# Rank products of a feed-forward group behind the eighth instead of the seventh first-layer step of the next group

## The chip, the cores and the metric

The kernel runs on one core of a Trainium2 chip. Five engines work side by side, each with its own queue in which instructions go in order: TensorE (PE: matrix products; weight loads are shown as PEld), VectorE (DVE), ScalarE (ACT), GpSimd (POOL) and SyncE (SP), which here only issues transfers. They wait for each other by semaphores. The metric is the time of one execution on the device in microseconds (us), and the median over several executions is compared.

## What is computed

The input is a graph with 1250 nodes of 512 features and 40000 edges. Cut to what matters:

```python
xn = _layernorm(x)
x = x + gnn(xn, W1, b1, W2, b2, eps, src, dst) + mix(xn)      # graph layer and attention
x = x + ffn(_layernorm(x))                                    # 16 experts, top 2

# gnn:  rst = (1 + eps) * feat + segment_sum(feat[src], dst)
#       h = relu(rst @ W1 + b1) @ W2 + b2;  return h + feat        (512 -> 1024 -> 512)
# ffn:  logits = xt @ router_w.T + router_b;  probs = softmax(logits)
#       topk_p, topk_i = top_k(probs, 2)
#       out = sum over experts e of gate_e * (gelu(xt @ w1e.T + b1e) @ w2e.T + b2e)
```

The change lies in the two dense layers of the graph layer, called the feed-forward here, and in the routing to the experts that is done beside them.

## The kernel before

The 1250 nodes are ten tiles of 128 rows. The kernel goes through stages: layer norm and projections, attention with the graph sums, the output projection, the feed-forward of the graph layer (about 438 to 567 us of the profiled execution), the rest of the routing, a loop over the experts' tiles, and the sum at the end. Every instruction's place in its queue is written out by hand, so the order on an engine is that of the code.

The feed-forward takes the tiles in four groups, FC_TILES: tiles 0 to 2, 3 to 5, 6 and 7, 8 and 9. For each group TensorE does the first layer in eight steps m = 0 to 7 (KH = 8), one for each 128 of the 1024 hidden features. A step is twelve products at line 1456: four slices of 128 inputs, three products each, since numbers are split into a high and a low part. They have 384, 256 or 226 columns, by the size of the group. A step writes one of four PSUM banks in turn and signals hid_ps. ScalarE makes h_32 and h_hi from it (lines 758 and 759), VectorE makes h_lo (line 1094). Then mix(t) does the second layer of a tile, 24 products of 512 columns at line 1399, which takes the h_lo of each step for the group's first tile. VectorE adds the result to the row (line 1107) and normalises it (lines 1109 to 1114), TensorE turns the normalised tile (turn_x2n, line 1408) and multiplies it by the router's weights (route, line 1417).

The routing of a group f - 1 is done during the first layer of group f, in pieces between the steps:

- TensorE does the last turning and router products behind steps 1 and 3.
- VectorE does pick(f - 1) behind the h_lo of step 4: sixteen small operations in a chain (lines 1021 to 1037), each waiting for the one before it. They find the two best experts of each row and write them to mask16. Line 1040 signals mask_ready.
- ScalarE does the exponents (line 744) behind step 5.
- TensorE does ranks(f - 1) at line 1424: small products that count, for each row and expert, how many earlier rows chose that expert. The first of them waits for mask_ready, the last signals rank_ps.
- VectorE does place, tally and weigh behind the h_lo of step 7. The first operation of place, line 1050, waits for rank_ps. Place writes the slots and signals slots_ready, on which GpSimd waits with its scatters (line 628). Tally updates seen, which the next ranks read.

The routing of the last group, tiles 8 and 9, has no steps beside it. It follows the last mix, and the expert loop follows that. SyncE loads eight experts' weights in the meantime: four when hid_ps has counted all 32 steps, four when mix_ps has counted ten tiles. It reads the first rows from the slots (line 457) when the scatters have landed.

Of the kernel before, what the change touches and what calls it, by code (L numbers as in the profile page):

```python
# [37 lines left out]
KH = HID // P  # L38
# [36 lines left out]
def layer(nc, x, src, dst, wqkv, wo, bo, gw1, gb1, gw2, gb2, geps, rw, rb, ew, eb1, eb2, out):  # L75
# [10 lines left out]
    with ExitStack() as ctx:  # L86
# [389 lines left out]
        def _(pool):  # L476
# [134 lines left out]
            for _, what, i in sorted([(start(max(w - 4, 0)), "cols", w) for w in range(NW)]  # L611
                                     + [(min(6 * (p + 1), RAW) + 0.5, "split", p) for p in range(2)]
                                     + [(summed[w // WPG], "spare", w) for w in range(0, NW, 2)]):
                {"cols": window_columns, "spare": spare_chunks, "split": split_pair}[what](i)
# [588 lines left out]
        def _(pe):  # L1203
# [91 lines left out]
            for g, (which, p, b) in enumerate(projections):  # L1295
                o, n = BLOCKS[b]
# [91 lines left out]
            def mix(t, first, hidden):  # L1388


                r = rows(t)
                c = (t - first) * P
                if t >= 2:
                    pe.wait_ge(x2_ready, t - 1)
                for m in range(KH):
                    if t == first:
                        pe.wait_ge(hid_lo, hidden + m + 1)
                    for i, (h, w) in enumerate(((h_hi, w2_hi[:, m, :]), (h_lo, w2_hi[:, m, :]), (h_hi, w2_lo[:, m, :]))):
                        ins = pe.matmul(bank[4 + t % 2][0:r, :], h[:, m, c:c + r], w,  # L1399
                                        start=(m == 0 and i == 0), stop=(m == KH - 1 and i == 2))  # L1400
                ins.then_inc(mix_ps, 1)

            def turn_x2n(t):
                pe.wait_ge(x2n_ready, t + 1)
                if t:
                    pe.wait_ge(x2nt_saved, t)
                for k in range(KD):
                    ins = pe.transpose(bank[6][:, k * P:(k + 1) * P], x2n[:, t, k * P:(k + 1) * P], ident[:, :])
                ins.then_inc(x2nt_ps, 1)

            def route(t):
                pe.wait_ge(x2nt_saved, t + 1)
                f = sum(1 for tiles in FC_TILES if tiles[-1] < t)
                if f and t == FC_TILES[f][0]:
                    pe.wait_ge(slots_ready, f)
                for k in range(KD):
                    ins = pe.matmul(bank[7][:, t * EXP:(t + 1) * EXP], x2n_t[:, t % 2, k, :], rw_sb[:, k, :],
                                    start=(k == 0), stop=(k == KD - 1))
                ins.then_inc(logit_ps, 1)

            def ranks(f):

                def ahead(to, of, mask, start, stop):
                    return pe.matmul(bank[7][:, to * EXP:(to + 1) * EXP], of[:, :], mask, start=start, stop=stop,
                                     skip_group_check=True)

                tiles = FC_TILES[f]
                masks = [mask16[:, t * EXP:(t + 1) * EXP] for t in tiles]
                pe.wait_ge(mask_ready, f + 1)
                for i, t in enumerate(tiles):  # L1430
                    ahead(NT + t, ones, seen[:, :], True, False)
                    for mask in masks[:i]:
                        ahead(NT + t, ones, mask, False, False)
                    ins = ahead(NT + t, tri, masks[i], False, True)
                if tiles[-1] == NT - 1:
                    ahead(2 * NT, ones, seen[:, :], True, False)
                    for mask in masks:
                        ins = ahead(2 * NT, ones, mask, False, mask is masks[-1])
                ins.then_inc(rank_ps, 1)
# [4 lines left out]
            for f, tiles in enumerate(FC_TILES):  # L1444
                o = tiles[0] * P
                n = min(N, tiles[-1] * P + P) - o
                for m in range(KH):
                    if g < 4:
                        pe.wait_ge(out_added, 4 + g)
                    else:  # L1450
                        pe.wait_ge(hid_hi, g - 3)
                    if g == 0 or g == KH // 2:
                        pe.wait_ge(w1_lo_ready, KD if g == 0 else 2 * KD)
                    for k in range(KD):
                        for i, (w, r) in enumerate(((w1_hi, rst_hi), (w1_hi, rst_lo), (w1_lo, rst_hi))):
                            ins = pe.matmul(bank[g % 4][:, 0:n], w[k][:, m * P:(m + 1) * P], r[k][:, o:o + n],  # L1456
                                            start=(k == 0 and i == 0), stop=(k == KD - 1 and i == 2))
                    ins.then_inc(hid_ps, 1)
                    g += 1

                    if o and m == 1:
                        turn_x2n(tiles[0] - 1)
                        route(tiles[0] - 2)
                    if o and m == 3:
                        route(tiles[0] - 1)
                    if o and m == 6:
                        ranks(f - 1)
                pe.wait_ge(w2_lo_ready, KH)
                pe.wait_ge(out_added, NT)
                for t in tiles:  # L1470
                    mix(t, tiles[0], g - KH)
                    if t - 1 in tiles:
                        turn_x2n(t - 1)
                    if t - 2 in tiles:
                        route(t - 2)
# [106 lines left out]
```

## Time and profile before

| | |
|---|---|
| Median of 3 runs | 740.73 us |
| Lowest and highest | 739.47 and 741.41 us |
| Profiled execution: time | 739.14 us |
| Profiled execution: span of the instructions | 737.4 us |
| Busy share of the span: TensorE, VectorE, ScalarE, GpSimd | 93%, 64%, 32%, 21% |
| Mean granted clock of TensorE | 0.972 of full |

The profile is of one execution. Its times are microseconds from the start of the span, so two places are compared by subtracting their starts. The time of an execution is its span plus 1.7 us around it. A busy share is an average over stages that are bound by different things, and what a stall costs is read at its own place: what the engine waits for, and what had stood ready to run. In the timeline a bracket behind a row gives the engine's idle time ahead of it and what ended it.

### The profile page before, as it was taken

To read this page: it belongs to the slowest core of one execution; us is meant where nothing else is said; L and a number is where in the kernel's file an instruction comes from. 1 tells how busy PE (TensorE), PEld (TensorE's weight loads), DVE (VectorE), ACT (ScalarE), POOL (GpSimd) and SP (SyncE) were. 2 spreads that over 40 slices of the span, in tenths; PEclk is the share of its full clock that TensorE was granted. 3 is DMA by queue.
4 is the path that set the end of the run, shared out by engine and by line. 5 is a ranking of instruction groups with operands and counts; after the bars stand their busy time and mean duration, and the time that the engine had idled before them with its cause. 6 is when DMAs were issued, how large, how long until landed. Compare 5 with 4: busy or idle time off the path is not lost.

```text
span 737.4 us, 12476 instructions
## 1 busy us (share of the span) xinstructions
PE 683.9 (93%) x3860; PEld 453.2 (61%) x3861; DVE 474.6 (64%) x1065; ACT 233.5 (32%) x472; POOL 155.9 (21%) x262
## 2 busy tenths in 40 slices
PE   4889999999999999999999999999898299999997
PEld 2545545455655565555555789898886176777742
DVE  5629752389888898887964997344445634445536
ACT  2222311223233232332333435160542243354320
POOL 6045210103133331312300700003112212232210
PEclk9999999999999999999999999999999589999978
DMA  9700000072543717090735920002018668844458
GB/s 292 212 0 0 1 3 1 0 288 102 204 171 133 258 46 286 22 342 30 276 137 184 382 112 1 1 1 87 17 70 315 263 205 300 307 142 127 130 201 301
DMA packets 48198, 109.70 MB, mean 149 GB/s; under 512 B 6694, under 2 KB 6710, under 8 KB 45680
## 3 DMA queue, kind: packets, MB, share of 16 engines
q1 hardware_dynamic: 38480, 85.41, 32.4%
q0 software_dynamic: 4256, 13.41, 4.9%
q10 hardware_dynamic: 5376, 9.93, 4.4%
q8 instruction: 31, 0.51, 0.3%
q14 instruction: 55, 0.45, 0.2%
HBM read 47.39 MB, written 61.35 MB: 147 GB/s over the span
## 4 chain that ended last, share of the span: by engine, by line
PE 80%; DVE 9%; DMA 3%; issue 3%; ACT 1%; POOL 1%; SPq 1%; DVEq 0%; ACTq 0%; POOLq 0%
PE bank L1361 12%; PE bank L1344 10%; PE bank L1312 8%; PE bank L1399 8%; PE bank L1278 7%; PE bank L1456 6%; PE bank L1522 6%; PE bank L1508 6%; PE bank L1323 5%; PE bank L1242 4%; PE bank L1384 4%; DMA arena<-in_x 2%; DVE arena L918 2%; PE bank L1532 2%; PE bank L1483 1%
## 5 line engine op out<-in xcount | busy, mean ns | idle before, releaser
L918 DVE TENSOR_TENSOR arena<-iota,arena 125x384 f16<-125x384 f16 (+2 forms) x318 | 172.6, 605 | 23.3 <-PE bank L1242 14.0
L718 ACT ACTIVATE arena<-bank 128x416 f32<-128x416 f32 (+1 forms) x120 | 62.2, 518 | 147.0 <-PE bank L1344 144.0
L1361 PE MATMUL bank<-arena 128*64 128x416 f32 (+1 forms) x480 | 97.2, 524 | 3.3 <-DVE arena L971 2.8
L971 DVE TENSOR_SCALAR arena<-bank 128x416 f32<-128x416 f32 (+1 forms) x120 | 67.5, 589 | 42.8 <-PE bank L1344 42.7
L554 POOL COPY arena<-arena 125x12 f32 (+1 forms) x80 | 35.2, 440 | 229.1 <-DVE arena L918 122.7
L1312 PE MATMUL bank<-arena 128*128 128x416 f32 (+1 forms) x192 | 75.8, 544 | 2.6 <-ACT arena L656 1.4
L1242 PE MATMUL bank<-arena 125*128 125x160 f16 x471 | 51.5, 234 | 5.7 <-DVE arena L918 5.2
L1508 PEld LDWEIGHTS bank<-arena 128*128 128x128 f32 x448 | 52.8, 194 | 6.2 <-issue 6.2
L1312 PEld LDWEIGHTS bank<-arena 128*128 128x128 f32 x192 | 36.7, 200 | 30.1 <-issue 26.7
L1242 PEld LDWEIGHTS bank<-arena 125*128 125x128 f16 x471 | 32.5, 98 | 36.8 <-issue 27.1
L1361 PEld LDWEIGHTS bank<-arena 128*64 128x64 f32 x480 | 30.6, 135 | 36.5 <-issue 26.7
L1508 PE MATMUL bank<-arena 128*128 128x128 f32 x448 | 52.9, 277 | 0.0
L1522 PE MATMUL bank<-arena 128*128 x112 | 50.4, 593 | 0.0
L628 POOL DMA_INDIRECT slots<-arena,slot x20 | 19.9, 996 | 140.1 <-DVEq L1057 135.2
L1153 DVE COPY arena<-arena 128x1024 f32 x30 | 20.9, 696 | 44.4 <-issue 40.2
L1344 PE MATMUL bank<-q_hi,k_hi 64*128 64x416 f32 (+1 forms) x240 | 48.7, 402 | 0.4 <-ACT arena L700 0.4
L638 POOL DMA_INDIRECT expert_rows<-arena x28 | 27.5, 980 | 97.6 <-DVE arena L1187 93.3
L1344 PEld LDWEIGHTS bank<-q_hi,k_hi 64*128 64x128 f32 x240 | 22.2, 181 | 39.3 <-issue 38.5
L1278 PE MATMUL bank<-xn_hi,a_t 128*128 128x512 f32 x100 | 45.5, 455 | 0.0
L1344 PE MATMUL bank<-q_lo,k_hi 64*128 64x416 f32 (+1 forms) x240 | 42.5, 350 | 0.0
L1344 PE MATMUL bank<-q_hi,k_lo 64*128 64x416 f32 (+1 forms) x240 | 42.4, 348 | 0.0
L1456 PE MATMUL bank<-rst_hi,w_hi 128*128 128x384 f32 (+2 forms) x128 | 40.3, 315 | 0.0
(247 smaller groups left out, 1183.6 us busy)
## 6 DMA issues: line engine op xcount, KB each, us to landing
slots<-arena SPq DMA_DIRECT2D x6, 5397.0 KB, 17.8
arena<-in_ew SPq DMA_DIRECT2D x16, 1024.0 KB, 6.0
slots<-arena SPq DMA_DIRECT2D x2, 5140.0 KB, 17.0
arena<-slots ACTq DMA_DIRECT2D x28, 257.0 KB, 3.0
arena<-in_x SPq DMA_DIRECT2D x8, 512.0 KB, 7.2
arena<-in_gw SPq DMA_DIRECT2D x2, 2048.0 KB, 17.0
arena<-in_wqkv SPq DMA_DIRECT2D x3, 1024.0 KB, 15.3
xn_rows<-arena SPq DMA_DIRECT2D x1, 2560.0 KB, 8.4
```

What stands on the lines that cost most here:

```text
L718: act.activation(probs[0:kt, s % NPB, 0, 0:n], bank[2 * (s % 2)][0:kt, 0:n], ACT.Relu).then_inc(p0_ready, 1)
L918: ins = dve.tensor_tensor(hot[:, :, c], iota16[0:CE, 0:width].unsqueeze(1).to_broadcast([CE, n, width]), window_cols[:, i % WBUF, of, k0:k ...
L971: dve.tensor_single_scalar(probs[0:kt, s % NPB, 1, 0:n], bank[2 * (s % 2) + 1][0:kt, 0:n], 0.0, op=ALU.max).then_inc(p1_ready, 1)
L1242: return pe.matmul(window_at(w), of[:, at_slot:at_slot + P], of[:, at_slot + P:at_slot + OHW], start=start, stop=stop, skip_group_check=True)
L1278: ins = pe.matmul(bank[NB][:, :], a_t[:, g % 2, t, :], x[t][:, :], start=(t == 0 and x is xn_hi), stop=(t == NT - 1 and x is xn_lo), skip_ ...
L1312: ins = pe.matmul(bank[g % 5][:, 0:n], w_qkv[:, part, k, c:c + P], xn_t[:, k, o:o + n], start=(k == 0), stop=(k == KD - 1))
L1344: ins = pe.matmul(bank[2 * (s % 2) + a][0:kt, 0:n], k[p][half, t * P:t * P + kt], q[p][half, o:o + n], start=(i == 0), stop=(i == len(term ...
L1361: ins = pe.matmul(bank[AV][DH * a:DH * a + DH, 0:n], v_sb[0:kt, t, h * DH:h * DH + DH], probs[0:kt, s % NPB, a, 0:n], start=(t == 0), stop ...
L1399: ins = pe.matmul(bank[4 + t % 2][0:r, :], h[:, m, c:c + r], w, start=(m == 0 and i == 0), stop=(m == KH - 1 and i == 2))
L1456: ins = pe.matmul(bank[g % 4][:, 0:n], w[k][:, m * P:(m + 1) * P], r[k][:, o:o + n], start=(k == 0 and i == 0), stop=(k == KD - 1 and i == 2))
L1508: ins = pe.matmul(bank[a][:, m * P:(m + 1) * P], w1_now[:, a, k * DFF + m * P:k * DFF + m * P + P], xg_t[:, a, k, :], start=(k == 0), stop ...
L1522: ins = pe.matmul(bank[6 + a][:, :], hg_t[:, a, k, :], arena[:, bass.ds(lies[a] + KD * DFF + k * D, D)], start=(k == 0), stop=(k == KF - 1))
```

## The change

```diff
@@ -1463,7 +1463,7 @@
                         route(tiles[0] - 2)
                     if o and m == 3:
                         route(tiles[0] - 1)
-                    if o and m == 6:
+                    if o and m == KH - 1:
                         ranks(f - 1)
                 pe.wait_ge(w2_lo_ready, KH)
                 pe.wait_ge(out_added, NT)
```

The call of ranks(f - 1) goes from behind the seventh step (m = 6) to behind the eighth (m = 7). That happens at three places, in the first layers of the groups of tiles 3 to 5, 6 and 7, and 8 and 9 (o is zero in the first group, which has no ranks to do). The orders of VectorE, ScalarE, GpSimd and SyncE stay word for word the same.

TensorE at the first place, tiles 3 to 5. The names rst_hi, rst_lo, w_hi and w_lo are the parts of the inputs and of the first layer's weights; a bracket names the semaphores that a row waits for. Rows with a minus stand there in the kernel before.

```order
 L1456 MATMUL bank<-rst_lo_109,w_hi_97 128x384
 L1456 MATMUL bank<-rst_hi_105,w_lo_101 128x384
-L1424 MATMUL bank<-seen,ones 128x16 [waits mask_ready]
-L1424 MATMUL bank<-mask,tri 128x16
-L1424 MATMUL bank<-seen,ones 128x16
-L1424 MATMUL bank<-mask,ones 128x16
-L1424 MATMUL bank<-mask,tri 128x16
-L1424 MATMUL bank<-seen,ones 128x16
-L1424 MATMUL bank<-mask,ones 128x16 x2
-L1424 MATMUL bank<-mask,tri 128x16
 L1456 MATMUL bank<-rst_hi_102,w_hi_94 128x384 [waits hid_hi]
 L1456 MATMUL bank<-rst_lo_106,w_hi_94 128x384
```

The ranks stood between the last product of the seventh step and the first of the eighth, which itself waits only for hid_hi.

TensorE at the third place, tiles 8 and 9, now, behind the twelve products of the eighth step. Rows with a plus are new there; w_hi and h_hi of line 1399 are the second layer.

```order
 L1456 MATMUL bank<-rst_lo_109,w_hi_97 128x226
 L1456 MATMUL bank<-rst_hi_105,w_lo_101 128x226
+L1424 MATMUL bank<-seen,ones 128x16 [waits mask_ready]
+L1424 MATMUL bank<-mask,tri 128x16
+L1424 MATMUL bank<-seen,ones 128x16
+L1424 MATMUL bank<-mask,ones 128x16
+L1424 MATMUL bank<-mask,tri 128x16
 L1399 MATMUL bank<-w_hi,h_hi 128x512 [waits x2_ready,hid_lo,out_added,w2_lo_ready]
 L1399 MATMUL bank<-w_hi,h_lo 128x512
```

The ranks and their wait now stand ahead of the second layer. The second place is moved in the same way.

VectorE at the first place, the same in both kernels: the end of pick, the h_lo of steps 5, 6 and 7, and the start of place.

```order
L1037 TENSOR_TENSOR mask<-arena 128x48 [waits dve_chain]
L1094 TENSOR_TENSOR h_lo<-arena,h_hi 128x384 [waits dve_chain,hid_hi]
L1094 TENSOR_TENSOR h_lo<-arena,h_hi 128x384 [waits hid_hi] x2
L1050 TENSOR_TENSOR arena<-bank,ebase 128x48 [waits rank_ps]
L1051 TENSOR_TENSOR arena<-arena 128x48 [waits dve_chain]
```

Place stands behind the h_lo of the eighth step, so it waits for that step as well as for the ranks.

## Rows read from the trace of the kernel before

**Rows 1.** The page: its first line, and the shares of the chain of waits.
```profile
span 737.4 us, 12476 instructions
...
PE 80%; DVE 9%; DMA 3%; issue 3%; ACT 1%; POOL 1%; SPq 1%; DVEq 0%; ACTq 0%; POOLq 0%
```

**Rows 2.** Who waited for whom, TensorE, 485 to 590 us (total, times, longest).
```profile
PE bank L1424 <- DVEq L1040: 8.2, 4, 3.7
```

**Rows 3.** Timeline, TensorE, first place (start, us, engine, line, operation, [idle before <-releaser]).
```profile
490.84 0.34 PE L1456 MATMUL bank<-rst_hi,w_lo 128*128 128x384 f32 x1
492.04 0.18 PE L1424 MATMUL bank<-seen,ones 128*128 128x16 bf16 x1 [0.86 <-DVEq L1040]
...
492.27 0.42 PE L1456 MATMUL bank<-rst_hi,w_hi 128*128 128x384 f32 x1
...
494.46 0.40 PE L1399 MATMUL bank<-w_hi,h_hi 128*128 128x512 f32 x1
```

**Rows 4.** Timeline, VectorE, first place.
```profile
491.71 0.21 DVE L1037 TENSOR_TENSOR mask<-arena 128x48 bf16<-128x48 f32 x1
...
495.75 0.56 DVE L1094 TENSOR_TENSOR h_lo<-arena,h_hi 128x384 fp32r<-128x384 f32 x1 [2.49 <-ACT h_hi L759]
496.22 0.20 DVE L1050 TENSOR_TENSOR arena<-bank,ebase 128x48 f32<-128x48 f32 x1
```

**Rows 5.** Timeline, TensorE, second place.
```profile
524.90 0.28 PE L1456 MATMUL bank<-rst_hi,w_lo 128*128 128x256 f32 x1
527.07 0.18 PE L1424 MATMUL bank<-seen,ones 128*128 128x16 bf16 x1 [1.89 <-DVEq L1040]
...
527.32 0.36 PE L1456 MATMUL bank<-rst_hi,w_hi 128*128 128x256 f32 x1
...
528.82 0.40 PE L1399 MATMUL bank<-w_hi,h_hi 128*128 128x512 f32 x1
```

**Rows 6.** Timeline, TensorE, third place.
```profile
551.98 0.28 PE L1456 MATMUL bank<-rst_hi,w_lo 128*128 128x226 f32 x1
553.99 0.18 PE L1424 MATMUL bank<-seen,ones 128*128 128x16 bf16 x1 [1.73 <-DVEq L1040]
...
554.13 0.35 PE L1456 MATMUL bank<-rst_hi,w_hi 128*128 128x226 f32 x1
...
555.55 0.41 PE L1399 MATMUL bank<-w_hi,h_hi 128*128 128x512 f32 x1
```

**Rows 7.** Timeline behind the last second-layer product, all engines.
```profile
566.91 0.69 DVE L1107 TENSOR_TENSOR arena<-arena,bank 98x512 f32<-98x512 f32 x1 [2.65 <-PE bank L1399]
...
587.58 1.48 SPq L457 DMA_DIRECT2D arena<-slots  x2
...
590.32 1.08 PE L1483 MATMUL bank<-ident,arena 128*128 128x128 f32 x4 [9.89 <-DMA arena<-slots]
```

**Rows 8.** Busy time of each engine in 1 us windows; PEclk is the granted clock.
```profile
569.00:570.00 1.00, 0.15 (x2) 0.09 (x2) 0.71 (x2) 0.07 (x1) 0.00 (x0) 0.93 0.94 390
...
593.00:594.00 1.00, 1.00 (x7) 1.00 (x7) 0.06 (x1) 0.40 (x1) 0.00 (x0) 0.62 0.08 16
```

**Rows 9.** Timeline, TensorE, around the two changes of the clock.
```profile
567.99 1.06 PE L1417 MATMUL bank<-rw_sb,arena 128*128 128x16 f32 x8 [0.69 <-ACT arena L770]
...
571.71 1.89 PE L1417 MATMUL bank<-rw_sb,arena 128*128 128x16 f32 x8 [0.69 <-ACT arena L770]
...
592.56 4.31 PE L1508 MATMUL bank<-arena 128*128 128x128 f32 x32
```

**Rows 10.** Chain of waits (start, us, what): second layer, expert loop, end.
```profile
494.62 11.10 PE bank L1399 x48
...
619.88 3.57 PE bank L1508 x32
...
719.11 3.73 PE bank L1546 x4
...
724.31 0.69 DVE arena L1199
```

## The prediction

> **What bounds the kernel now.** I read the page first. The chain of waits, followed back from the last instruction, lies 80% on TensorE and only 9% on VectorE [rows 1]. So TensorE is what a change has to make shorter, and what matters is where TensorE stands still. The next view is therefore the list of who waited for whom, for TensorE alone, from 485 us, in the first layer of tiles 3 to 5, to the expert loop. Its largest entry is line 1424, the rank products, which waited four times, 8.2 us in all, and the longest wait was 3.7 us [rows 2]. What released them was VectorE's queue at line 1040, the signal at the end of pick. The longest of the four is that of the last ranks, those of tiles 8 and 9, which have no step behind them and are not touched by the change. That leaves about 4.5 us for three waits, and the timelines show them: 0.86, 1.89 and 1.73 us of idle time ahead of the first rank product [rows 3, 5, 6].
>
> These three stalls are a real loss and not slack that something else covers. Between the waits TensorE runs without a gap: the last product of the seventh step starts at 490.84, then nothing starts until 492.04, although the eighth step (line 1456) needs nothing from pick. It stands behind the rank products only because the queue is in order. Behind it the second layer (line 1399) starts at 494.46 and keeps the array busy for 11.10 us, 48 products without a gap [rows 10].
>
> **The change part by part.** Nothing is added or removed. At three places, in the first layer of tiles 3 to 5, of tiles 6 and 7 and of tiles 8 and 9, the rank products (eight, eight and five rows of the order) move from ahead of the eighth first-layer step to behind it. The wait on mask_ready moves with them. On VectorE, ScalarE, GpSimd and SyncE the order stays. So each place is a matter of three times: when the seventh step ends, when the mask is there, and how long the eighth step takes.
>
> First place, tiles 3 to 5. The last product of the seventh step starts at 490.84 and its successors follow each other about 0.175 us apart: from 492.27 to 494.46 are twelve products, of which the first has some 0.1 us more. So TensorE could have gone on at 491.02. It went on at 492.04 [rows 3], a stall of 1.02 us. With the change the eighth step starts at 491.02 and needs 2.09 us, to 493.11. The last operation of pick runs from 491.71 to 491.92 [rows 4], so the mask is there 1.1 us before the rank products come up, and they wait for nothing. The gain is the whole stall: **1.02 us**.
>
> Second place, tiles 6 and 7. The seventh step's last product starts at 524.90, and TensorE is free at 525.02. The ranks started at 527.07, 2.05 us later. The eighth step lasts 1.50 us from 527.32 to 528.82 [rows 5], of which 0.08 is the slower start after a pause. It now ends at 526.44, and the mask comes at the same time as before, since what pick waits for (line 1094 of the fifth step and the router products ahead of it) isn't moved. So 0.63 us of waiting are left. The ranks then run from 527.07 and take 0.25 us, and the second layer starts at 527.32 to 527.40 where it was 528.82. The gain is not the stall but the length of the step put into it: **1.42 us**.
>
> Third place, tiles 8 and 9. TensorE is free at 552.09, the ranks start at 553.99, and the step goes from 554.13 to 555.55 [rows 6]. The step has 1.34 us without its slow start. It ends at 553.43, 0.56 us of waiting are left, and the second layer starts at 554.13 to 554.21. Gain: **1.34 us**.
>
> The sum is 1.02 + 1.42 + 1.34 = 3.78 us. If the slow start of 0.08 us isn't paid by the second layer, it is 3.94, so I take **3.8 us**.
>
> **What could become late instead.** Four things hang on the moved products or on the step.
> Place (line 1050) waits for the ranks. At the first place these end 1.1 us later than before, at about 493.4 us. But VectorE did not come to line 1050 before 496.22, since the h_lo of the eighth step stands ahead of it and was made at 495.75 [rows 4]. That h_lo now comes 1.3 us earlier, because the step no longer stands behind stall and ranks: still about 1.4 us behind the ranks. The cover holds. At the other two places the ranks start when they did, so nothing is later.
> The second layer's first tile takes h_lo step by step. It takes the eighth h_lo seven steps behind its start, and a step has three products of 11.10 / 48 = 0.23 us [rows 10], so 4.8 us behind it, by my reckoning at 498.1 at the first place. The h_lo is there at about 495.0. Were this cover gone, every microsecond would be paid by TensorE.
> The eighth step uses the bank that the fourth step's ScalarE reads have left long before.
> The slots come from place, and with it the scatters of GpSimd. Both get earlier.
>
> Downstream, the gain has to come through to the end. Behind the last second-layer product the chain goes over VectorE (line 1107 had stood idle for 2.65 us waiting for TensorE, at 566.91), the routing of the last tiles, the scatters, and then SyncE's read of the slots at 587.58, for which TensorE stood idle 9.89 us until 590.32 [rows 7]. All these wait for products that now end 3.8 us earlier. So do the first eight loads of expert weights: SyncE issues them at the last hid_ps and the last mix_ps. I find no transfer that starts by another event than these and ends in this stretch, so the whole tail should slide. Nothing new is hidden or uncovered by it.
>
> **The clock.** The granted clock is 2.4 GHz at the three places and falls to 1.2 GHz during the window from 569 to 570 us (mean 0.93 there), after pauses of TensorE in the routing of the last tiles. It rises again in the window from 593 to 594 (mean 0.62) [rows 8]. The eight router products took 1.06 us ahead of the fall and 1.89 behind it [rows 9]. The stalls that the change removes were at full clock and cost no clock, so none is won back there.
> The Trainium skill (TensorE: Matmul & The Clock Gate, Part 1: The HAM clock gate) says that the gate looks at activity in windows that run freely, not in step with the kernel. By that rule the slide of the work against the windows may let the fall and the rise meet other products. The trace neither confirms nor denies it, as it shows one execution.
>
> **The rivals.**
> *Full gain* (the forecast): 3.8 us, 740.73 - 3.8 = 736.9.
> *Absorbed gain.* The end is set somewhere behind by something that doesn't move, as a transfer of weights or rows in the tail. For it speaks that TensorE waits 9.89 us for the slots' read [rows 7] and that transfers are in the chain with 3% [rows 1]. Against it speaks that I find an event of TensorE or VectorE ahead of each of them. A partial form: only the first stall's 1.02 us or only half of the sum comes through. That gives 738.8 to 740.7.
> *Slower by the clock.* The mechanism is one: the low level holds more of the work behind 567 us than now. Its price from rows: thirty-two products of the expert loop take 3.57 us at the full clock [rows 10], 4.31 when the rise falls among them [rows 9], and would take about 7.1 entirely at the low level: 2.8 us more. An earlier fall would take the router products of the tile before it with it, 1.89 - 1.06 = 0.83 more [rows 9]. At the end two tiles of line 1546 take 3.73 us at the low level [rows 10], 1.86 each, while behind the rise the chain lies on VectorE, with two operations of about 0.69 for a tile, one of which is shown. Eight tiles kept low cost 8 x (1.86 - 1.38) = 3.8 us. All together 7.4 us, so 740.73 - 3.8 + 7.4 = 744.3. It decides for slower only from 6.0 us on, since 3.8 must be eaten first and 2.2 are 0.3%. It needs all three places at once. One alone only makes the gain smaller, and the opposite case (a late fall, 0.8 us, or an early rise, 0.7 us) makes it larger.
> *The change does nothing.* It would need that TensorE already runs the eighth step during the wait. The starts at 490.84 and 492.04 with nothing between exclude it [rows 3].
>
> **How the numbers follow.** The sum is made against the profiled execution: span 737.4, time 739.14, which gives 733.6 and 735.3. That execution lies 1.6 us under the median of the runs shown, 740.73. The runs themselves span 739.47 to 741.41, which I read as the size of what the clock and the transfers do by chance, about 1 us to each side. For the median I take 740.73 - 3.8 = 736.9. Chances: full gain, with that scatter, 0.84. Absorbed in part or whole, 0.12. Slower by the clock, 0.04. A measurement of this kernel can tell about 0.3%, 2.2 us, from no change: faster means under 738.5, slower over 742.9. From the full case a small part with an unlucky clock falls within 0.3%, and a part of the absorbed case ends under 738.5, and the two about cancel. A little of the slow case stays under 742.9 too. So faster 0.84, same 0.13, slower 0.03. The range goes from 734.9 (the sum of 3.94, with 1.9 us more from an early rise, a late fall and the scatter of the runs) to 739.2, which takes in half of the absorbed case.
>
> **What the changed kernel's profile would show.** At the first place the rank products without idle time ahead of them, behind the twelve products of the eighth step; in the second and third an idle time of about 0.6 us ahead of the ranks. The wait list of TensorE for line 1424 should fall from 8.2 us to 3.7 + 0.6 + 0.6 = 4.9. The second layers should start at 493.4, 526.3 and 551.7 us (the earlier gains taken off: 1.0 at the second, 2.4 at the third), and the last second-layer product should end at 563.1. The place of line 1050 should still be released by VectorE's own order and not by line 1424. The prediction is wrong in its core if the second layer starts as early as this and the span doesn't follow, and wrong in the sum if the mask comes later than before relative to the fifth step.

## The result

The changed kernel takes 735.29 us (median of 5 runs, 732.79 to 737.21), the kernel before 740.73 us (median of 5, 739.47 to 743.22). The ratio is 0.9917 with a 95% interval of 0.9892 to 0.9943, so the change saves 4.2 to 8.0 us, with 5.4 between the medians. The forecast was 3.8 us, with a range of 734.9 to 739.2 us. The direction was right, and the local mechanism too, but the size lies above it: 3.8 us would be a ratio of 0.9949, just outside the interval, and the ratio of 0.9917 on 740.73 us gives 734.6, just under the range, though the median itself lies in it. Medians and intervals leave out executions more than 1.5% above the fastest of their kernel, which is a single one, of 756.32 us in e2.

The page of the changed kernel, its first line and the shares of the chain of waits, beside [rows 1]:

```profile
span 735.5 us, 12476 instructions
...
PE 80%; DVE 8%; DMA 4%; issue 3%; ACT 1%; POOL 1%; ACTq 1%; SPq 0%; DVEq 0%; POOLq 0%
```

The profiled execution (737.21 us) is the longest of its five, and the profiled one of before (739.14) was the shortest seen until then. Their spans differ by 1.9 us only. Which of the two numbers, 1.9 or 5.4, the change made is what the rest is about.

TensorE's waits from 485 to 590 us, beside [rows 2]:

```profile
PE bank L1424 <- DVEq L1040: 4.6, 3, 3.7
```

8.2 us in four waits have become 4.6 in three, and the 3.7 of the last tiles are still among them. The forecast was 4.9.

The executions already differ ahead of the change. To compare, one needs a place that both share, and I take the first product of the second layer of tiles 0 to 2, which the change does not touch. In the kernel before:

```profile
455.56 0.50 PE L1399 MATMUL bank<-w_hi,h_hi 128*128 128x512 f32 x1 [0.29 <-DVE w_lo L1091]
```

TensorE in the changed kernel, the same place and then the three places of the change, beside [rows 3, 5, 6]:

```profile
456.35 0.50 PE L1399 MATMUL bank<-w_hi,h_hi 128*128 128x512 f32 x1 [0.29 <-DVE w_lo L1091]
...
493.92 0.18 PE L1424 MATMUL bank<-seen,ones 128*128 128x16 bf16 x1
...
494.16 0.48 PE L1399 MATMUL bank<-w_hi,h_hi 128*128 128x512 f32 x1
...
526.86 0.18 PE L1424 MATMUL bank<-seen,ones 128*128 128x16 bf16 x1 [0.45 <-DVEq L1040]
...
527.12 0.47 PE L1399 MATMUL bank<-w_hi,h_hi 128*128 128x512 f32 x1
...
552.36 0.18 PE L1424 MATMUL bank<-seen,ones 128*128 128x16 bf16 x1 [0.39 <-DVEq L1040]
...
552.58 0.48 PE L1399 MATMUL bank<-w_hi,h_hi 128*128 128x512 f32 x1
```

The changed execution is 456.35 - 455.56 = 0.79 us late before it comes to the change. That taken off, the second layers start at 493.37, 526.33 and 551.79, where they started at 494.46, 528.82 and 555.55: earlier by 1.09, 2.49 and 3.76 us, which is 1.09, 1.40 and 1.27 us for the three places. The forecast was 1.02, 1.42 and 1.34. At the first place the ranks no longer wait, at the other two the rest of the wait is there. The first product of the second layer now takes 0.48 or 0.47 us where it took 0.40, so this layer pays for the slower start behind the ranks.

VectorE at the first place, beside [rows 4]:

```profile
492.51 0.21 DVE L1037 TENSOR_TENSOR mask<-arena 128x48 bf16<-128x48 f32 x1
...
495.20 0.56 DVE L1094 TENSOR_TENSOR h_lo<-arena,h_hi 128x384 fp32r<-128x384 f32 x1 [1.14 <-ACT h_hi L759]
495.67 0.20 DVE L1050 TENSOR_TENSOR arena<-bank,ebase 128x48 f32<-128x48 f32 x1
```

Place still comes behind the h_lo of the eighth step, 1.4 us behind the ranks' end at about 494.2, and waits for nothing else. The cover that the prediction named holds.

Behind the second layer, all engines, beside [rows 7]:

```profile
564.01 0.69 DVE L1107 TENSOR_TENSOR arena<-arena,bank 98x512 f32<-98x512 f32 x1 [2.65 <-PE bank L1399]
...
584.68 1.48 SPq L457 DMA_DIRECT2D arena<-slots  x2
...
587.46 1.09 PE L1483 MATMUL bank<-ident,arena 128*128 128x128 f32 x4 [9.92 <-DMA arena<-slots]
```

From the common place to this addition it is 107.66 us, and was 111.35: **3.69 us** saved, the 3.76 less that slower start. From the addition to the read of the slots it is 20.67 us in both, so the stretch behind slides as a whole. The gain that can be seen in the two traces is thus 3.7 us. The rest of the way the two executions differ by things that the change does not touch: 0.79 us at the start, 0.09 less up to the expert loop, 0.68 more in the loop and 0.41 more behind it. The sum, 0.79 - 3.69 - 0.09 + 0.68 + 0.41, is the -1.9 us of the spans.

So two questions were left: where single executions get their noise of several microseconds, and why the medians say more than 3.7.

### The profile page after: what moved, and what is told of

It reads as the page before. It is cut to its first block, busy times and chain, and to the rows that moved or that the text cites. A ratio compares the mean times of both kernels' runs of the same rounds, so it can differ in the third digit from the quotient of the medians.

```text
span 735.5 us, 12476 instructions
## 1 busy us (share of the span) xinstructions
PE 685.5 (93%) x3860; PEld 453.7 (62%) x3861; DVE 473.5 (64%) x1065; ACT 233.7 (32%) x472; POOL 153.4 (21%) x262
## 4 chain that ended last, share of the span: by engine, by line
PE 80%; DVE 8%; DMA 4%; issue 3%; ACT 1%; POOL 1%; ACTq 1%; SPq 0%; DVEq 0%; POOLq 0%
PE bank L1361 12%; PE bank L1344 10%; PE bank L1312 9%; PE bank L1399 8%; PE bank L1278 7%; PE bank L1456 6%; PE bank L1522 6%; PE bank L1508 5%; PE bank L1323 5%; PE bank L1242 4%; PE bank L1384 4%; DMA arena<-slots 2%; DVE arena L918 2%; DMA arena<-in_wqkv 2%; PE bank L1532 2%
## 5 line engine op out<-in xcount | busy, mean ns | idle before, releaser
L918 DVE TENSOR_TENSOR arena<-iota,arena 125x384 f16<-125x384 f16 (+2 forms) x318 | 169.7, 593 | 23.3 <-PE bank L1242 14.0
L554 POOL COPY arena<-arena 125x12 f32 (+1 forms) x80 | 33.3, 417 | 230.8 <-DVE arena L918 136.1
L1312 PEld LDWEIGHTS bank<-arena 128*128 128x128 f32 x192 | 37.3, 203 | 31.0 <-issue 27.3
```

Source lines behind the costliest of these rows:

```text
L918: ins = dve.tensor_tensor(hot[:, :, c], iota16[0:CE, 0:width].unsqueeze(1).to_broadcast([CE, n, width]), window_cols[:, i % WBUF, of, k0:k ...
L1312: ins = pe.matmul(bank[g % 5][:, 0:n], w_qkv[:, part, k, c:c + P], xn_t[:, k, o:o + n], start=(k == 0), stop=(k == KD - 1))
```

## The experiments

Theory A says that the gain is 3.7 us and the rest chance. Theory B says that the expert loop gives a surplus. Theory C came up with the second experiment: TensorE's stalls cost clock as well as time. Each comparison is with runs of the kernel before on the same chip in the same job.

**e1, the changed kernel once more.**

> The changed kernel once more, to see how firm its gain of 5.4 us (median) is. Theory A (the gain is the 3.8 us at the three places and the rest is chance, since the first reads of rows in the expert loop land late by different amounts from execution to execution): 3 to 5 us under the kernel before, a profile whose second layers start 1.0 to 1.1, 2.4 to 2.5 and 3.7 to 3.8 us earlier relative to the first layer's start. Theory B (the change also spares about 2 us in the expert loop): again 5 to 6 us under it, with the first passes of the loop shorter in the profile than in the kernel before.

Measured: 736.73 us (8 runs, 733.82 to 740.44) against 741.17 (15 runs), ratio 0.9929 (0.9901 to 0.9957), so 4.4 us between the medians. The profile has the same local times: 107.69 us from the common place to the addition. But it is a long execution, with a span of 738.7 us, and its chain of waits shows two things. It comes to the common place 2.0 us later than that of before (457.51), and the reads of rows in the expert loop are late. The chain in the loop, start, time, what; first e1, then the first changed execution:

```profile
597.46 3.44 PE bank L1522 x8
...
607.51 8.04 DMA arena<-slots
...
616.70 4.62 PE bank L1522 x8
```

```profile
592.01 3.00 DMA arena<-slots
...
605.99 6.31 DMA arena<-slots
...
623.23 6.10 DMA arena<-slots
```

A read of rows takes 3.0 us ahead of the loop and 6.1 to 8.0 us when SyncE loads expert weights of 1 MB beside it. Then the pass waits. A pass without a wait is 7.88 us long; over the loop's thirteen intervals the excess is 2.1 us in the profile of before, 2.8 in the changed one and 4.7 in e1. That speaks against theory B, under which the changed kernel's loop would be shorter, and names one source of noise. Another is the common place itself, which comes anywhere between 454.5 and 458.3 us in the profiles.

The wait costs e1 clock as well. TensorE stood idle for 2.80 us ahead of the pass at 615.6 us, and the granted clock is low over that pass, so the eight products at 616.70 take 4.62 us instead of 3.44:

```profile
614.00:616.00 2.00, 0.41 (x2) 0.42 (x3) 0.17 (x1) 0.00 (x0) 0.00 (x0) 0.89 0.16 66
616.00:618.00 2.00, 2.00 (x6) 1.17 (x5) 0.65 (x1) 0.60 (x1) 0.00 (x0) 0.50 0.82 211
```

**e4, the changed kernel with the loads of weights spread over the passes.**

```diff
-            for e in (6, 7, 8, 11, 12, 13, 14, 15):
+            for i, e in enumerate((6, 7, 8, 11, 12, 13, 14, 15)):
+                if i:
+                    sp.wait_ge(y_ps[1], i)
                 expert(e)
```

> The changed kernel with the expert weights that are loaded during the expert loop spread over the passes: each load after the first waits for the end of one more pass's last product. The reads of rows then don't share the transfer engines with 1 MB loads. Theory A: the reads land in about 3 us instead of 6 to 7, no pass of the loop is longer than 7.9 us, 1.5 to 3 us under the changed kernel, and the runs lie within 2 us where those of the changed kernel lay within 4.4. Rival (the reads are late for another reason): passes of about 9 us remain and the time stays.

Measured: 731.96 us (5 runs, 731.55 to 733.26), ratio 0.9873 (0.9839 to 0.9906), 4.8 us under e1. All passes are 7.88 us long, and no transfer is left in the chain of the loop:

```profile
595.38 3.44 PE bank L1524 x8
598.81 3.57 PE bank L1510 x32
602.38 0.87 PE bank L1485 x8
603.26 3.44 PE bank L1524 x8
```

The gain is larger than the 1.5 to 3 us expected, and fits e1's profile with its 4.7 us of excess better than the first one with 2.8. The runs lie within 1.7 us, those of e1 within 6.6. The late reads came from the loads beside them.

**e2, the ranks one step earlier (unspread).** It is the opposite of the change: `if o and m == 5:`.

> The ranks one step earlier than in the kernel before, behind the sixth step (m = 5). Theory A: each stall grows by one step, 2.09 + 1.42 + 1.34 = 4.85 us, and all of it reaches the end: 740.7 + 4.9 = about 745.6. In the profile the idle times ahead of the ranks are about 3.0, 3.4 and 3.1 us. Rival (something behind the feed-forward takes up the slide): less than 3 us. Theory B: more than 6 us.

Measured: 748.52 us (7 runs), 7.4 over the kernel before; the ratio, 1.0087 (1.0056 to 1.0118), gives 6.4, or 4.2 to 8.7. The middle lies above theory A's 4.85 and at theory B's 6, but the interval still takes in 4.85. What decides is the profile. TensorE at the first place, and the granted clock around it (the column third from the end, 1.00 for 2.4 GHz and 0.50 for 1.2):

```profile
491.99 0.20 PE L1424 MATMUL bank<-seen,ones 128*128 128x16 bf16 x1 [2.96 <-DVEq L1040]
...
499.14 0.39 PE L1399 MATMUL bank<-w_hi,h_hi 128*128 128x512 f32 x1
```

```profile
488.00:490.00 2.00, 1.03 (x6) 0.71 (x5) 1.66 (x7) 0.95 (x3) 0.00 (x0) 1.00 0.00 0
490.00:492.00 2.00, 0.01 (x1) 0.02 (x2) 1.63 (x10) 1.65 (x3) 0.00 (x0) 0.79 0.00 0
492.00:494.00 2.00, 2.00 (x15) 2.00 (x16) 0.56 (x1) 0.00 (x0) 0.00 (x0) 0.50 0.03 8
...
498.00:500.00 2.00, 2.00 (x12) 1.88 (x11) 0.12 (x1) 0.66 (x2) 0.00 (x0) 1.00 0.00 0
```

The stall is the expected one, 2.96 us. But during it the clock goes from 2.4 to 1.2 GHz and stays there until 498 us, so the next step and most of the one behind it run at half speed. From the common place to this second layer it is 43.63 us instead of 38.90: 4.7 us for a step of 2.1. At the other two places it is 2.9 and 2.8 us for 1.4 and 1.3, with the clock low from about 532 and 563 us. Each stall of 3 us cost 1.5 to 2.6 us more than itself. That is theory C: it was not among the prediction's rivals for these places.

**e3, the ranks one step later.** They go into mix(t), behind the first three products of the group's first tile.

```diff
-                    if o and m == KH - 1:
-                        ranks(f - 1)
@@ in mix(t, first, hidden, f)
+                    if t == first and first and m == 0:
+                        ranks(f - 1)
```

> The ranks one step later than in the changed kernel, behind the first three products of the second layer's first tile, at the same three places. Theory A: the idle times of 0.45 and 0.39 us that the changed kernel's profile shows ahead of the ranks at the second and third place are covered by these products (0.69 us), so 0.8 us under the changed kernel. Rival (place on VectorE now waits for the ranks): idle time ahead of line 1050's operation with the ranks as its releaser, and no gain or a loss.

Measured: 735.15 us (6 runs), ratio 0.9916 (0.9883 to 0.9949), 1.6 under e1, which the intervals don't separate. In the profile the waits are gone at all three places. The second one, TensorE:

```profile
525.58 0.40 PE L1399 MATMUL bank<-w_hi,h_hi 128*128 128x512 f32 x1
...
526.29 0.18 PE L1426 MATMUL bank<-seen,ones 128*128 128x16 bf16 x1
```

From the common place to the addition it is 106.44 us, 1.2 less than in the changed kernel. 0.84 of them are the two waits.

**e5 and e6, the kernel before and the changed one, both with spread weights.** The loop's noise is taken out of the comparison.

> The kernel before with the same spread of the expert weights as in e4. The passes of the expert loop are then equal in both kernels, and the difference to e6 is that of the moved ranks alone. Theory A (only the stalls count): 3.7 us over e6, as the profiles say. Theory C (a stall of 2 us of TensorE lets its clock fall in some executions, as one of 3 us did in e2): 4 to 6 us over e6, and among the runs some with a mean clock lower by 0.002 to 0.004 that are longer by 1 to 3 us. Rival B (the loop gave the surplus): the difference is 3.7 and the runs lie close together.

> The kernel of e4 once more, on the chip of e5. All theories: 731.5 to 732.5 us on this scale, with all passes of the loop 7.88 us long and runs within 2 us.

Measured: 737.60 us (9 runs, 736.22 to 739.09) and 733.04 (6 runs, 729.87 to 734.93); ratios to the kernel before 0.9918 (0.9889 to 0.9946) and 0.9853 (0.9813 to 0.9893). The change is worth 4.6 us between the medians and 4.8 between the means, and by the scatter of the two sets of runs the latter is 3.2 to 6.4. So 3.7 is not excluded by this pair. The loop cannot give a surplus here, as all its passes are 7.88 us long in both profiles, so rival B is out. The mean clock of the runs is 0.9704 in e5 and 0.9720 in e6, a difference within their scatter. And e5's profile shows the full clock at all three places, so theory C was not shown yet. The runs of e6 spread over 5 us, more than the 2 expected, and their median is 0.5 us over the expected 731.5 to 732.5.

**e7 and e8, spread weights with the ranks later, and earlier.**

> Ranks behind the first three products of the second layer (as e3) and spread weights (as e4). The local gain of e3's profile over the changed kernel's, 1.2 us between the first second layer and the last add, should now be visible in the time: 1.2 us under e6 (0.8 from the idle times, the rest from fewer slow starts). If the median is within 0.4 us of e6, the local gain doesn't come through.

> Ranks behind the sixth step (as e2) and spread weights (as e4). Theory A alone: 4.85 us over e5. Theory C: e2's profile lost 2.6, 1.5 and 1.5 us more at the three places, since the clock fell behind each stall of 3 us, so 9 to 10.5 us over e5, and a mean clock lower by 0.006 to 0.01.

Measured: e7 730.96 us (6 runs, 729.32 to 735.25), ratio 0.9839 (0.9797 to 0.9881). It is 2.1 us under e6 by the medians and 1.2 by the means, and 1.35 by the traces (106.44 against 107.79 us from the common place to the addition). The interval does not exclude that it is no better than e6. e8 747.67 us (12 runs), 10.1 over e5, where the local stalls alone would be 4.85; its mean clock is 0.962. Its profile has a low clock behind each of the three stalls of 2.96, 3.31 and 3.07 us. Theory C holds for stalls of 3 us, in six of six cases with e2.

**e9 to e12, between the two, and place by place.** e9 has the ranks in the middle of the seventh step, e10 is e5 again, e11 keeps only the first place's stall, e12 only the other two.

```diff
@@ e9: in the loop over k of line 1456's products, behind them
+                        if o and m == 6 and k == 1:
+                            ranks(f - 1)
@@ e11
-                    if o and m == 6:
+                    if o and m == (6 if f == 1 else 7):
@@ e12
-                    if o and m == 6:
+                    if o and m == (7 if f == 1 else 6):
```

> Spread weights, and the ranks in the middle of the seventh step (behind its second slice of inputs). Each stall is half a step longer than in e5: about 2.1, 2.8 and 2.6 us. The local sum without any fall of the clock is 1.05 + 0.71 + 0.67 = 2.4 us over e5. Theory A: that. Theory C (stalls of 2 to 3 us let the clock fall in a part of the executions): 4 to 6 us over e5, a mean clock between those of e5 and e8, and a profile in which one or two of the three stalls are followed by a stretch at the low clock.

> The kernel of e5 once more on this chip, as the ground for e9, e11 and e12. 737 to 738.5 us. Theory C: with stalls of 1.0, 2.1 and 1.9 us a fall behind one of the last two stands in some profiles; the chance that this one shows it is about a third to a half.

> Spread weights, and the ranks moved at the second and third place only, so that the first place keeps its stall of 1.0 us. Locally 2.6 us under e10 (1.40 + 1.27). Theory A: 2.6 under it. Theory C: the surplus hangs on the two stalls of 2 us, so 3.5 to 4.5 under e10 and a mean clock as of e6 (0.972).

> Spread weights, and the ranks moved at the first place only, so that the second and third keep their stalls of 2.1 and 1.9 us. Both theories: 1.1 us under e10, since the stall of 1.0 us costs only itself. Under theory C the mean clock stays that of e5 and e10 (0.970). A gain of 2 us or more here would say that the surplus sits at the first place.

| | median us (runs) | ratio to before | mean clock | common place to addition |
|---|---|---|---|---|
| e10 | 739.01 (12) | 0.9957 (0.9922 to 0.9991) | 0.968 | 111.47 |
| e9 | 740.22 (12) | 0.9972 (0.9937 to 1.0007) | 0.970 | 115.32 |
| e11 | 731.76 (6) | 0.9850 (0.9805 to 0.9894) | 0.976 | 108.69 |
| e12 | 735.89 (8) | 0.9916 (0.9877 to 0.9956) | 0.972 | 110.51 |

The traces give what was expected of the places: e12 saves 0.96 us, e11 saves 2.78. The times say more, 3.1 and 7.3 us, which neither theory expected. The expectation of e12 had named a sign for a gain of 2 us or more: that the surplus sits at the first place, with its stall of 1.0 us. The 3.1 us are such a gain, but with this scatter they are 1.0 to 5.1, and no profile shows a fall behind that stall. e10 itself came out 1.4 us over e5, the same kernel, and its twelve runs reach from 736.2 to 745.7 us, so part of these two differences may be e10's.

e11 and e12 can be compared without e10. They differ in which stalls they keep, e11 the first and e12 the other two, and e12 takes 4.1 us more by the medians and 4.3 by the means (2.7 to 5.9), where the traces give 110.51 - 108.69 = 1.8. Its mean clock is 0.972 against 0.976. So the executions with the two stalls of 2 us lose more than the stalls, and show a lower clock, although the one profile of e12 has no fall at either place. How much of the clock's difference lies at these places is not shown: in the two profiles the low stretch behind the routing of the last tiles also differs, 23.9 us in e12 and 20.5 in e11.

In e9 the 3.85 us of the trace are 2.4 of longer stalls and one fall of the clock, behind the stall of 2.60 us at the second place; behind those of 1.91 and 2.41 us there is none. By the medians e9 is only 1.2 us over e10, less than either theory said. The runs of e9 fall apart in two: seven with a mean clock of 0.972 to 0.975 take 738.1 to 740.5 us, five with 0.963 to 0.967 take 741.8 to 745.4.

e9, the granted clock behind the stall of 2.60 us:

```profile
526.00:528.00 2.00, 0.00 (x0) 0.00 (x0) 1.72 (x11) 1.59 (x3) 0.00 (x0) 1.00 0.00 0
528.00:530.00 2.00, 1.50 (x18) 1.50 (x19) 0.77 (x3) 0.20 (x1) 0.00 (x0) 0.87 0.00 0
530.00:532.00 2.00, 2.00 (x11) 2.00 (x11) 0.43 (x1) 0.64 (x2) 0.00 (x0) 0.50 0.00 0
```

**e13 to e16, four further profiles of e5's kernel.** What was left was whether the stalls of 2 us, those that the kernel before has, do it too.

> A profile of the kernel of e5. Theory C: in about a third of such profiles the granted clock is low for some microseconds right behind the ranks of the second or third place, the second layer behind it starts 1 to 2 us later, and the time is over 739 us. Rival (chance elsewhere): full clock there in every profile; long executions are long at the start, in the routing of the last tiles or at the end.

> As e13, a further profile: theory C a fall behind a stall of 2 us in one of three, the rival none.

> As e13, a further profile: theory C a fall behind a stall of 2 us in one of three, the rival none.

> As e13, a further profile: theory C a fall behind a stall of 2 us in one of three, the rival none.

They do in all four profiles, where theory C expected one in about three. TensorE and the granted clock in e13, at the second place:

```profile
526.54 0.18 PE L1426 MATMUL bank<-seen,ones 128*128 128x16 bf16 x1 [1.90 <-DVEq L1042]
...
528.53 0.63 PE L1401 MATMUL bank<-w_hi,h_hi 128*128 128x512 f32 x1
```

```profile
524.00:526.00 2.00, 0.64 (x6) 0.44 (x4) 1.72 (x11) 1.97 (x5) 0.00 (x0) 1.00 0.00 0
526.00:528.00 2.00, 1.46 (x19) 1.47 (x20) 1.15 (x4) 0.39 (x2) 0.00 (x0) 0.99 0.00 0
528.00:530.00 2.00, 2.00 (x8) 1.71 (x7) 0.36 (x2) 1.22 (x3) 0.00 (x0) 0.50 0.00 0
530.00:532.00 2.00, 2.00 (x8) 1.59 (x7) 1.65 (x12) 0.91 (x1) 0.50 (x1) 0.66 0.00 0
```

And e10, the same kernel with the same stall (1.89 us, ranks at 528.23), without a fall:

```profile
528.00:530.00 2.00, 1.77 (x22) 1.78 (x23) 0.88 (x3) 0.08 (x1) 0.00 (x0) 1.00 0.00 0
530.00:532.00 2.00, 2.00 (x11) 1.65 (x10) 0.89 (x5) 1.81 (x3) 0.00 (x0) 1.00 0.00 0
```

In e13 the fall comes late, when TensorE is already busy with the eighth step, and lies over the second layer, whose 512-column products then take 0.63 us instead of 0.39. So it isn't seen in the stall itself. In e14 it comes earlier, from about 526.5 us, right behind the stall. The mean clock of the stretches around the second and the third place, in e13 and then in e14:

```profile
520.00:545.00 25.00, 23.11 (x145) 20.34 (x144) 12.43 (x49) 7.63 (x17) 5.77 (x6) 0.93 0.17 64
545.00:566.00 21.00, 19.27 (x125) 17.27 (x125) 9.87 (x44) 9.31 (x21) 3.85 (x4) 0.92 0.33 120
```

```profile
520.00:545.00 25.00, 23.10 (x146) 20.55 (x144) 12.40 (x49) 7.74 (x16) 5.77 (x6) 0.93 0.17 64
545.00:566.00 21.00, 19.27 (x129) 16.73 (x129) 10.59 (x46) 8.93 (x20) 3.85 (x4) 1.00 0.42 155
```

e15 is like e14, with a fall behind the second stall only, and e16 like e13, with both. In time: from the first place's second layer to the addition it is 72.45 us in the profile of before, 73.99 and 74.01 in e14 and e15, 75.62 and 75.61 in e13 and e16. Each fall costs 1.55 to 1.6 us.

The whole times don't show it by themselves. They are 739.48, 737.64, 740.56 and 738.55 us, so e14 and e16 stay under the 739 us that theory C expected of a profile with a fall, while the profiled executions of e5 and e10, without one, took 737.60 and 738.34. Other differences hide the falls: three of the four came to the common place at 454.5 to 455.0 us, e5 and e10 at 457.1 and 456.7.

Counted over the profiles of all kernels that have the stalls of 2.1 and 1.9 us (before, e5, e10, e12 to e16): a fall behind the second place in four of eight, behind the third in two of eight. All six are in e13 to e16, which ran on one chip in one job; the other four profiles, from other jobs, have none. So the falls are shown, but how often they come is not: it may depend on the chip or the job. Behind the first place's stall of 1.0 us there is none in the eight profiles that have it (e12 out, e11 in). In the six profiles with the ranks moved at all three places (the changed kernel, e1, e3, e4, e6, e7) the clock is full from 485 us to the last product of the second layer.

## Why the prediction was right and where it was wrong

- **What bounds the kernel, and that the stalls are real loss:** right. The slide of 3.69 us goes unchanged to the read of the slots. Behind it other differences of the single executions mix in. From the common place to the end of the span it is 281.8 us before and 279.2 after, 2.7 less, and with spread weights 278.8 in e5 and 275.8 and 275.9 in e4 and e6, 3.0 less of 3.6.
- **The sum at the three places:** 1.02, 1.42 and 1.34 forecast, 1.09, 1.40 and 1.27 in the trace. The rests of the waits were put at 0.6 us and are 0.45 and 0.39 in idle time; the ranks themselves start as computed, the difference is the tail of the last product, which the view counts as busy. The prediction left open whether the second layer pays the slower start of 0.08 us behind the ranks (3.78 or 3.94 us). It does.
- **The covers** (place behind the ranks, h_lo ahead of the second layer): they held.
- **The step that failed is the one on the clock.** The prediction said: "The stalls that the change removes were at full clock and cost no clock, so none is won back there." That was true of the one profiled execution and not of the kernel. In the eight profiles with these stalls, that of before among them, the clock falls behind them in six of sixteen cases, at 1.57 us each, where the prediction's term was nothing. On average that is 6 x 1.57 / 8 = 1.2 us in an execution, a rough estimate, since four profiles of one job have all six falls (2.4 us each on average) and the other four have none. With 1.2 the change is worth 3.7 + 1.2 = 4.9 us. Measured were 5.4, 4.4 and 4.6 between the medians of three comparisons, with 4.2 to 8.0, 3.2 to 7.3 and 3.2 to 6.4 around them, and 4.9 is inside all three. 3.7 is outside the first only; the differences of the means, weighted by their scatter, give 5.1 us together, 4.0 to 6.2, which leaves 3.7 out by a little. That the falls make the surplus fits with this and with e11 against e12, but the two profiles with these stalls that were taken beside the three comparisons (before and e5) have no fall at these places, so this last step is argued. The profiled execution of before was among the shortest, which was a hint: a sum made against it leaves out what it happened to be spared.
- The page that the prediction cites (the Trainium skill, TensorE: Matmul & The Clock Gate, Part 1: The HAM clock gate) says that the gate's windows run freely. The prediction drew from it only that the falls after 567 us could move. By the same rule one stall can meet a window badly in one execution and not in another, and e10 and e13, the same kernel without and with a fall, agree with that; the windows themselves are shown by no run. The prediction could have had this as a rival, with a price from rows: the second layer at half speed for a few microseconds.
- **The rivals:** none of the three came in its full size. Nothing absorbed the gain. The low stretch that begins at 564 to 575 us has 23.9 us in the profiles before and after, so it did not get longer there. But its length varies: it is 27.3 us in three of the six profiles with all three ranks moved (e1, e4, e6) and in one of the eight with the stalls of 2 us (e13), and then the way from the addition to the first pass of the loop is 0.8 us longer (32.4 us on average instead of 31.6). So the clock's rival was right that the length varies, and whether the change makes the longer stretch likelier is not settled. The reading that the scatter of the runs, about 1 us to each side, is the clock's and the transfers' was right in kind and too small in size: later runs of the kernel before reach from 737.2 to 747.7 us.
- **Not settled:** the gains of e11 and e12 against e10 are larger than their traces, and whether the first stall, of 1.0 us, has a part in that. No profile of a long execution of e10 was taken (its runs go up to 745.7), so what makes these long is not shown. Falls of the clock are also seen in places the change doesn't touch, as at 411 to 415 us in e1, e8 and e15.

The best version that was run is e7, with the ranks inside the second layer and the weights' loads spread over the passes: 730.96 us, a ratio of 0.9839 (0.9797 to 0.9881) to the kernel before. Most of what it gains over the change comes from the spread loads.

## What to carry to other kernels

An in-order queue loses the smaller of two times when a waiting instruction stands ahead of work that is ready: the stall, or the length of the work that can be put ahead of it. So first move ready work ahead until the wait is used up, and check who waits for what was moved behind. Price a TensorE stall of 2 us or more not only by its length but also by a possible fall of the clock behind it, even where the profile at hand shows none: one profile is one draw, so take several, from more than one job, before a sum rests on "the clock is full here". Bulk loads that aren't urgent should not be issued beside small reads that the next pass waits for.

## What the runs showed of the hardware

- A TensorE stall in an otherwise busy stretch let the granted clock fall from 2.4 to 1.2 GHz behind it in none of eight cases at 1.0 us, in six of seventeen at 1.9 to 2.1 us (the sixteen above and e9's first), in e9 behind 2.6 but not behind 2.4, and in all six at 3.0 to 3.3 us (lengths by the view's idle times, or up to 0.2 us more between starts). The six falls behind stalls of about 2 us are all in the four profiles of one job (e13 to e16). Behind the 2.80 us of idle time in e1's loop it fell too, and the eight products behind it took 4.62 us instead of 3.44. A fall behind a stall of 2 us cost 1.57 us, one behind 3 us cost 1.5 to 2.6.
- The fall can come after TensorE is busy again (528 us in e13, with the stall ending at 526.5), so it lies over work that has nothing to do with the stall. It can also come right behind it (526.5 us in e14).
- Reads of 257 KB of rows took 3.0 us alone and 6.1 to 8.0 us beside loads of 1 MB. Spreading eight such loads over the passes of the loop brought the changed kernel from 736.73 to 731.96 us, and the kernel before from 741.74 to 737.60 and, on another chip, from 742.18 to 739.01. The spread of the changed kernel's runs went from 6.6 to 1.7 us, but was 5.1 again in e6, and e10's twelve runs reach over 9.6 us. In e14 and e15 one pass each was still 0.4 and 0.8 us too long.
